# First of four convolutions computed directly ahead of a composed filter, in a two-layer style-convolution kernel

## The reference, cut to what matters

```
x = x + ffn0(cond0(x, style))      # ffn0 is a product with a 1024 x 1024 matrix
x = x + ffn1(cond1(x, style))      # ffn1 adds a gated low-rank part (LoRA experts)

cond: four convolutions of 3 taps, 64 -> 64 channels, in a row:
  same (1024) -> upsample x2 and blur [1,3,3,1] -> same -> blur and downsample x2
each: s = style @ mw.T + mb
      weight = SCALE * w * s[:, None, :, None]
      weight *= rsqrt(sum(weight * weight) + EPS)     # one factor per sample and output channel
      out = conv(x, weight) + bias
```

## Time and profile before

| what | value |
|---|---|
| time, median of 3 runs | 1484.66 us |
| profiled execution: span of its instructions | 1481.5 us |
| PE / weight loads (PEld) busy | 98% / 93% |
| DVE / ACT / POOL busy | 67% / 49% / 31% |
| granted PE clock | 1.00 of full speed but for the opening (0.91 from 20 to 40 us) |
| DMA | 145 MB, 36% of 16 queues' span |

### The profile page before, as it was taken

One profiled execution on the slowest core, in us unless ns is written; L12 is line 12 of the kernel. 1 busy time (PEld: TensorE's weight loads), 2 busy tenths in 40 slices (PEclk: granted clock), 3 DMA queues, 4 the chain that ended last, 5 costly groups with the idle time before them and its releaser, 6 DMA issues.

```text
span 1481.5 us, 28220 instructions
## 1 busy us (share of the span) xinstructions
PE 1457.1 (98%) x9619; PEld 1370.7 (93%) x9619; DVE 992.7 (67%) x2355; ACT 719.4 (49%) x1618; POOL 465.1 (31%) x542
## 2 busy tenths in 40 slices
PE   6999999999999999999989999999999999999999
PEld 4889898988988898889879999999999999999998
DVE  8766667766566655555676677677677677677674
ACT  5455445555544554455444445445454454454452
POOL 4133233323323332333313233233233233232230
PEclk9999999999999999999999999999999999999999
DMA  6443433443243234323533423423424424324322
GB/s 134 108 110 77 114 101 78 114 116 101 72 114 104 80 101 113 106 76 101 142 122 78 113 69 100 113 65 104 113 60 110 112 58 113 109 61 113 107 63 71
DMA packets 56635, 145.14 MB, mean 98 GB/s; under 512 B 19365, under 2 KB 21861, under 8 KB 56586
## 3 DMA queue, kind: packets, MB, share of 16 engines
q1 hardware_dynamic: 55928, 144.19, 36.2%
q10 hardware_dynamic: 658, 0.30, 0.1%
HBM read 110.92 MB, written 33.55 MB: 98 GB/s over the span
## 4 chain that ended last, share of the span: by engine, by line
PE 95%; DVE 3%; DMA 0%; issue 0%; SPq 0%; POOL 0%; ACT 0%; DVEq 0%; POOLq 0%; ACTq 0%
PE bank L1564 48%; PE bank L1416 13%; PE bank L1418 13%; PE bank L1417 13%; PE bank L1724 4%; PE bank L1596 1%; PE bank L1585 1%; PE bank L1629 1%; PE bank L1658 0%; DMA ends<-in_x_dram 0%; DVE win L1159 0%; DVE mtmp L1158 0%; PE bank L1741 0%; PE bank L1647 0%; DVE fw_l L1153 0%
## 5 line engine op out<-in xcount | busy, mean ns | idle before, releaser
L1564 PE MATMUL bank<-fw_h,ct_h 128*128 128x354 f32 (+2 forms) x1256 | 448.0, 357 | 0.8 <-DVE xout L1124 0.8
L1564 PE MATMUL bank<-fw_l,ct_h 128*128 128x354 f32 (+2 forms) x1256 | 445.1, 354 | 0.0
L1564 PE MATMUL bank<-fw_h,ct_l 128*128 128x354 f32 (+2 forms) x1256 | 443.2, 353 | 0.0
L414 POOL COPY conv_buf<-edge 128x4 f32 (+1 forms) x128 | 21.2, 193 | 848.9 <-DVE tw L1251 835.0
L1564 PEld LDWEIGHTS bank<-fw_h,ct_l 128*128 128x128 f32 x1256 | 236.1, 188 | 21.3
L1564 PEld LDWEIGHTS bank<-fw_h,ct_h 128*128 128x128 f32 x1256 | 236.7, 188 | 17.6 <-DVE ct_l L1275 0.9
L1564 PEld LDWEIGHTS bank<-fw_l,ct_h 128*128 128x128 f32 x1256 | 236.5, 188 | 15.5
L405 POOL TENSOR_TENSOR d_l<-d_f,d_h 128x512 fp32r<-128x512 f32 x128 | 154.8, 1209 | 102.4 <-ACT d_h L634 102.2
L1416 PE MATMUL bank<-d_h,tw 128*128 128x256 f32 x640 | 181.8, 284 | 0.3 <-DVE beta L974 0.3
L1418 PE MATMUL bank<-d_h,tw 128*128 128x256 f32 x640 | 180.5, 282 | 0.0
L1417 PE MATMUL bank<-d_l,tw 128*128 128x256 f32 x640 | 180.0, 281 | 0.0
(11 more groups left out here) (246 smaller groups left out, 3114.6 us busy)
## 6 DMA issues: line engine op xcount, KB each, us to landing
xraw<-in_x_dram SPq DMA_DIRECT2D x32, 512.0 KB, 6.6
xres<-in_x_dram SPq DMA_DIRECT2D x32, 512.0 KB, 4.2
x_dram<-xout SPq DMA_DIRECT2D x32, 512.0 KB, 2.9
xraw<-x_dram SPq DMA_DIRECT2D x32, 512.0 KB, 6.4
xres<-x_dram SPq DMA_DIRECT2D x32, 512.0 KB, 4.4
xraw<-in_x_dram SPq DMA_DIRECT2D x32, 511.5 KB, 8.0
xraw<-x_dram SPq DMA_DIRECT2D x32, 511.5 KB, 7.9
out_dram<-xout SPq DMA_DIRECT2D x31, 512.0 KB, 2.9
```

The costliest lines, as they stand in the source:

```text
L1564: last = mm(ffn_ps[e][:, 0:cols.stop - cols.start], ctf((ct_h, ct_h, ct_l)[part], k), (fw_h, fw_l, fw_h)[part][:, k, cols], start=k == beg ...
```

## The change

The first convolution is taken out of the composition and run over the sample by itself (`stage_mix`): two blocks of 128 rows, three matmuls of 512 columns each, so six matmuls of 512 columns a sample, into the whole of `conv_ps[h]`. `stage_t` goes. The composed filter holds the other three convolutions. It has seven taps in four slots (`NSH = 4`) and so six tap products of 256 columns a sample in `stage_conv` instead of eight.

The input of the filter is now the first convolution's result. ACT scales `xraw` by the style factor into a new tile `sig` (`x_scale`), casts its high part into the memory of `d_h` (`x_high`), POOL makes the low part (`split_low`); after `stage_mix` ACT scales PE's result back into `sig` (`mix_scaled`); POOL makes differences of it (`differ`), ACT the high parts (`y_high`), POOL the low parts (`lows`), and only then `stage_conv` can run. The filter's tile `t_f` is copied from PE's result by ACT (`f_high`) and DVE (`f_low`) with no scale, and has its own memory. A new list `x_take` puts ACT's scaling of the next pair between `t_high` and `sum_scaled`. SP's loads of `xraw` wait for `x_scaled`. In the opening of layer 0 DVE's `ends_2` and the third `prep_bias` change places, and the first `stage_conv` waits for all three biases.

```diff
-NSH = 5
+NSH = 4
...
+def halves(j, h, mixed=False):
+    return 4 * j + 2 * mixed + h + 1
...
                 def turn(j, first=False):
-                    sp.wait_ge(s["x_ready"], 2 * j)
+                    sp.wait_ge(s["x_scaled"], 2 * j)
                     load_x(ly, j)
...
+                def differ(h):
+                    m0, m1 = (sig[:, h, at:at + HL].rearrange("p (n e) -> p e n", e=2) for at in (0, 1))
+                    return nc.gpsimd.tensor_tensor(d_f[h][:, :, :], m0, m1, ALU.subtract)
+                def lows(h):
+                    nc.gpsimd.tensor_tensor(d_l[h][:, :, 1:QL + 1], d_f[h][:, :, :], d_h[h][:, :, 1:QL + 1].bitcast(F32), ALU.subtract)
+                    return nc.gpsimd.tensor_tensor(o_l[h][:, 1:QL + 1], sig[:, h, 1:HL:2], o_h[h][:, 1:QL + 1].bitcast(F32), ALU.subtract)
...
+                        pool.wait_ge(s["x_hi"], halves(j, h))
+                        nc.gpsimd.tensor_tensor(x_l[h], sig[:, h, :], x_h[h].bitcast(F32), ALU.subtract).then_inc(s["x_ready"], 1)
+                def mixed(j):
+                    for h in range(2):
+                        pool.wait_ge(s["y_made"], 2 * j + h + 1)
+                        differ(h).then_inc(s["d_made"], 1)
+                    for h in range(2):
+                        pool.wait_ge(s["x_hi"], halves(j, h, True))
+                        lows(h).then_inc(s["x_ready"], 1)
...
+            def x_scale(ly, j, h, before=None):
+                act.wait_ge(s["x_load"], 32 * j + 32)
...
+                    act.wait_ge(before["s"]["x_ready"], halves((j if before is ly else NPAIR) - 1, h, True))
+                nc.scalar.activation(sig[:, h, 0:HL], xraw[:, h, 0:L:2], ACT.Copy,
+                                     scale=ly["s_all"][:, 0, bass.ds(2 * j + h, 1)]).then_inc(s["x_scaled"], 1)
...
+                def mix_scaled(j, h):
+                    act.wait_ge(s["conv_acc"], halves(j, h))
+                    nc.scalar.activation(sig[:, h, 0:HL], conv_ps[h][:, :], ACT.Copy,
+                                         scale=lam1[:, bass.ds(2 * j + h, 1)]).then_inc(s["y_made"], 1)
...
-                    z_high(j)
+                    mix_scaled(j, 0)
+                    mix_scaled(j, 1)
+                    y_high(j, 0)
+                    f_high(j)
+                    y_high(j, 1)
                     t_high(j)
...
+                    x_take(j, 0, last)
+                    x_take(j, 1, last)
...
                 def t_low(j):
                     for h in range(2):
-                        v.tensor_scalar(full[:, 0:NSH, :], comp_ps[h][:, 0:NSH * C].rearrange("p (u c) -> p u c", c=C),
-                                        s_all[:, 0, bass.ds(2 * j + h, 1)], None, ALU.mult).then_inc(s["g_made"], 1)
...
+                        dve.wait_ge(s["f_dve" if h else "f_act"], 2 * j + 2)
+                        v.tensor_tensor(t_f[h][:, G0:SLOTS, :], t_f[h][:, 0:3, :], t_f[h][:, 1:4, :], ALU.add).then_inc(s["g_made"], 1)
...
+                def stage_mix(j, h, first=False):
+                    pe.wait_ge(s["x_ready"], halves(j, h))
+                    if not first:
+                        pe.wait_ge(s["ct_ready"], 4 * j)
...
+                    for i in range(2):
+                        at = slice(i * P, i * P + P)
+                        last = three(conv_ps[h][:, :], w1_h[:, at], w1_l[:, at], x_h[h][:, i:i + HL], x_l[h][:, i:i + HL], not i, bool(i))
+                    last.then_inc(s["conv_acc"], 1)
...
-                    for i, slot in enumerate((G0, G1, 4)):
+                    for i, slot in enumerate((G0, G1)):
...
                 def body(j, step=None):
                     stage_v(j)
                     ffn(ly, j - 1, 0, 9)
+                    stage_mix(j, 0)
+                    stage_mix(j, 1)
+                    ffn(ly, j - 1, 9, 12)
                     stage_u(j)
-                    ffn(ly, j - 1, 9, 19)
-                    stage_t(j)
-                    ffn(ly, j - 1, 19, 33)
+                    ffn(ly, j - 1, 12, 33)
                     stage_conv(j, 0)
                     stage_conv(j, 1)
...
                     ffn(ly, j - 1, 0, 13)
+                    stage_mix(j, 0)
+                    stage_mix(j, 1)
+                    ffn(ly, j - 1, 13, 17)
                     if not composed:
                         stage_u(j)
-                    ffn(ly, j - 1, 13, 28)
-                    if not composed:
-                        stage_t(j)
-                    ffn(ly, j - 1, 28, 49)
+                    ffn(ly, j - 1, 17, 49)
```

More of the change, by code:

```diff
@@ L360, in _ @@
                 if not n:
-                    sp.wait_ge(second["s"]["x_ready"], 2)
+                    sp.wait_ge(second["s"]["x_scaled"], 2)
                     load_x(second, 1)
@@ L455, in _ @@
                     ends_0()
-                for i, (full, hi, lo) in enumerate(((w3_st, w3_h, w3_l), (dn_st, dn_h, dn_l), (w1_st, w1_h, w1_l))):
-                    if i == 1 and not ly["lora"]:
-                        neighbours(0)
+                for i, (full, hi, lo) in enumerate(((w3_st, w3_h, w3_l), (sta[:, 4:8, :], w1_h, w1_l), (dn_st, dn_h, dn_l))):
                     pool.wait_ge(s["split_hi"], i + 1)
@@ L469, in _ @@
                 else:
-                    pool.wait_ge(s["t_ready"], 2)
-                    pool.wait_ge(s["t_side"], 2)
-                    neighbours(1)
+                    split_low(0)
+                    mixed(0)
                     pool.wait_ge(s["edge_ready"], 1)
@@ L715, in _ @@
                     fw_high(0, 2)
+                    x_high(ly, 0, 0)
+                    x_high(ly, 0, 1)
                     act.wait_ge(zs["scales_made"], 1)
                     v_high(0)
-                    x_high(ly, 0, 0)
-                    x_high(ly, 0, 1)
                     prep_m4(ly, (0, 1))
-                    z_high(0)
+                    act.wait_ge(zs["scales_made"], 2)
+                    mix_scaled(0, 0)
+                    mix_scaled(0, 1)
+                    f_high(0)
+                    y_high(0, 0)
+                    y_high(0, 1)
                     t_high(0)
@@ L1137, in _ @@
                         v.memset(tw[h][half(0), :, 0, 1, :].bitcast(F32), 0.0)
-                    v.memset(z_f[half(1), :, 3, :], 0.0)
+                    for h in range(2):
+                        v.memset(t_f[h][half(1), 3, :], 0.0)
                     link(v.memset(bb[:, :].bitcast(F32), 0.0))
@@ L1708, in stage_conv @@
                     last.then_inc(s["p_acc"], 1)
-                    if not first:
-                        pe.wait_ge(s["ct_ready"], 4 * j)
-                    elif not ly["lora"] and not h:
-                        pe.wait_ge(s["bias_ready"], 3)
-                    for i, slot in enumerate((0, 2, 4)):
-                        conv_tap(h, conv_ps[h][:, 0:QL], slot, d_h[h][:, 0, i:i + QL], d_l[h][:, 0, i:i + QL], i == 0, i == 2)
-                    for i, slot in enumerate((1, 3)):
-                        last = conv_tap(h, conv_ps[h][:, QL:2 * QL], slot, d_h[h][:, 1, i:i + QL], d_l[h][:, 1, i:i + QL], False, i == 1)
+                    for e in range(2):
+                        for i in range(2):
+                            last = conv_tap(h, conv_ps[h][:, e * QL:(e + 1) * QL], 2 * i + e, d_h[h][:, e, i:i + QL],
+                                            d_l[h][:, e, i:i + QL], not e and not i, i == 1)
```

214 lines of the change are left out of this document (104 added, 110 removed).

## The result

The changed kernel takes 1527.93 us (median of four runs, 1527.05 to 1532.84) against 1484.77 for the kernel before beside it (four runs, 1483.17 to 1485.86): +43.2 us, a ratio of 1.0299 (95% interval 1.0282 to 1.0316). The forecast was 1504 (+19.5): the direction is right, and less than half of the loss was seen.

The account below looks back on a forecast made before the run. PE, busy 98% of the span, was taken as the bound. On a span of 1481.5: -4 for PE's work, +20 hold at the filter run, +3 opening, 1500.5; with 3.2 to the median, 1504 us. Range 1481 to 1538 (by bounds 1484 to 1524).

Parts of the forecast that it names:

- PE's own work: PE's matmuls per pair: stage_t and two taps go, stage_mix comes; 0.06 us less a pair, -4 us over 64 pairs.
- the hold at the filter tile: Filter run: DVE's tile work held behind POOL; PE waits 0.45 us a body in layer 0, 0.2 in layer 1: +20 us.
- the opening: Opening of layer 0: the third bias comes after ends_2 and PE's first filter run waits for it: +3 us (0 to +5).
- the turn: PE's transposes of conv_buf: no term in the sum; rival 2 found 0.3 to 0.4 us to spare at 0.72 per scale.
- rival 2: At the turn ACT becomes the bound if each x_scale takes 0.5 us more: 0.6 a body, 1525 to 1545, chance 0.15.
- Its sign: What would show rival 2 in the profile: PE's transposes of conv_buf wait; no size given.
- the sum's own range: Range by the bounds of the terms around the forecast of 1504: 1484 to 1524 us.
- Rival 3: Mix matmuls on PE cost other than the ffn's: 0.01 us each is 8 us; no separate chance, the rest has 0.02.
- the 0.25 more of cover: Layer 1, between mix and filter run: 7.12 us of PE work against 6.87, so a wait of 0.2 (0 to 0.5).
- A difference: POOL's new differences of the mix result, reading with a step of 8 bytes: 1.27 us each (1.20 to 1.32).
- the low parts by themselves: POOL's low parts before the filter run: 2.07 us a sample, 4.1 for two, ending at 11.75 even alone.
- DVE adds 0.87 (614.28 to 615.07 and a tail): 18.7: Rival 2's step at the turn: after ACT's second sum at 17.8 DVE ends at 18.7; PE wants it at 19.0.

Follow-up runs that it names:

- e5: POOL's low parts (d_l, o_l) cut to two columns, on the changed kernel with w2_l after both conv_out: 1487.33 us, ratio 1.0021 to the kernel before.
- e1: Changed kernel, with DVE making the next pair's w2_l after both conv_out instead of between them: 1498.77 us, ratio 1.0102 to the kernel before.
- e3: Changed kernel, with ACT scaling the next pair's x after the first sample's sum and w2_high instead of ahead of them: 1499.03 us, ratio 1.0099.
- e2: Changed kernel, DVE's order left, with POOL making the next pair's x_l only after both conv_out of this pair: 1499.81 us, ratio 1.0105.
- e7: Changed kernel with x scaled after the first sum, two ffn matmuls moved ahead of the filter run, third bias before ends_2: 1486.43 us, ratio 1.0017.
- e6: Third bias ahead of ends_2, on the changed kernel with w2_l after both conv_out and two ffn matmuls moved: 1487.66 us, ratio 1.0027.

## Why the prediction was wrong

In the forecast's own terms the loss is: PE's own work -2 (forecast -4), the hold at the filter tile +9.6 (+20), the opening +3.8 (+3), and the turn +32, for which the sum had no term (by rival 2's sum 0.3 to 0.4 was to spare there). That makes 43.4, against 43.2 by the medians and 44.7 by the spans. The range of 1481 to 1538 holds 1528, and so does rival 2's band (1525 to 1545, chance 0.15), but by luck: that band came from `x_scale` at 1.2 us each. Its sign, PE's transposes of `conv_buf` that wait, did appear, but the hold of `w2_l` gives the same sign. By the bounds that it names, the sum's own range would begin at 1481, not at 1484.

**PE's own work: right in sign, half the size.** Mix matmuls start 0.233 apart (0.231 forecast). Undisturbed bodies are 21.11 (e5) and 22.27 us (e1), 0.02 and 0.04 less than before: -2 us, not -4. Rival 3 falls.

**The hold at the filter tile: right in kind, half the size.** PE wanted the tile at 12.45 in the body above (648.39, with the body's start at 635.94; forecast 12.42); it came at 12.54 (forecast 12.85) and PE was 0.31 late (forecast 0.45). In layer 1 the 0.25 more of cover sufficed: 0, not 0.2. The sum is 9.6 us, not 20. POOL's rows in that body, and then two where DVE had made the tile long before (pair 1 of layer 1), say which term was mis-sized:

```profile
642.60 1.04 POOL L404 TENSOR_TENSOR d_f<-sig 128x512 f32<-128x512 f32 x1 [0.37 <-ACT sig L686]
643.60 1.20 POOL L408 TENSOR_TENSOR d_l<-d_f,d_h 128x512 fp32r<-128x512 f32 x1
...
645.59 1.31 POOL L408 TENSOR_TENSOR d_l<-d_f,d_h 128x512 fp32r<-128x512 f32 x1
```

```profile
805.53 1.19 POOL L408 TENSOR_TENSOR d_l<-d_f,d_h 128x512 fp32r<-128x512 f32 x1
806.67 0.75 POOL L409 TENSOR_TENSOR o_l<-sig,o_h 128x256 fp32r<-128x256 f32 x1
```

The low parts begin 7.66 into the body (643.60), as forecast (7.65), but by luck. A difference takes 1.04, not 1.27, less than its lower bound of 1.20; but the second one waits 0.37 for ACT's second `mix_scaled`, a wait for which the prediction has no term, so the quicker row gains nothing. From there POOL took 4.39 us to the end of its last low part (647.99); the forecast was 4.1 and 0.6 for what DVE gets in between. The 0.6 was right: the two samples' `o_l` took 0.87 and 1.13 and the second `d_l` 1.31, where 0.75 and 1.19 are the rows with no DVE subtraction or addition let in. The mis-sized term is the low parts by themselves: 3.75 for the four (805.53 to 809.28), not 4.1. `o_l` was priced by a row that read `xraw` with a step of 16 bytes; it now reads `sig` with 8.

The 1.20 that was taken as a floor for the difference is a packed subtraction, but one that writes fp32r; no run here tells what the type of output costs by itself. The Trainium skill's GPSIMD Engine Reference (Performance pitfalls for Q7 kernels) had the direction right: with a step of 8 bytes in place of 16 the row fell from 1.32 to 1.04, so 16 was 27% dearer, where the page says half as much again. The page's figure is per element and ours is for the whole row, and a row is more than its elements (256 columns of `o_l` take 0.75, more than half of the 1.04 or 1.20 of 512), so the two need not differ.

**The turn: the step that failed.** Rival 2's sum put ACT's second sum at 17.8 and PE's wish at 19.0; they came at 17.5 and 18.9. `x_scale` was 0.75 (0.72 forecast; the rival had 0.5 more):

```profile
L605 ACT ACTIVATE sig<-xraw,s_all 128x512 f32<-128x512 f32 x128 | 90.3, 752 | 4.7 <-POOL o_l L409 1.6 <-issue 0.5
L686 ACT ACTIVATE sig<-bank,lam 128x512 f32<-128x512 f32 x128 | 88.0, 689 | 212.6 <-PE bank L1467 212.6
```

So ACT was in time for the second sum (rival 2 falls, as e3 shows), and the sentence "DVE adds 0.87 (614.28 to 615.07 and a tail): 18.7" is the error. It priced `conv_out` alone and left out what stands ahead of it on DVE: the `w2_l` pair, which had moved into the same microsecond as POOL's new x_l row. With it `conv_out` ended at 19.4. This cost some 31 us (32.0 of lateness at the turn, less the 0.9 that e1 leaves); e1, e2 and e3 each gave back 28 to 29. The row that would have shown it was in hand: the 1.53 us pair at 1102.44 is this very `w2_l`, held by POOL in this very place. The prediction used it to price the hold at the tile and did not ask why it cost nothing there. The trace of before answers:

```profile
1104.29 0.47 DVE L1268 SCALAR_TENSOR_TENSOR conv_buf<-bank,lam,conv_buf 128x254 f32<-128x254 f32 x1
```

```profile
1105.05 1.03 PE L1724 MATMUL bank<-ident,conv_buf 128*128 128x128 f32 x8
```

`conv_out` ended at 1104.76, and the second four transposes were wanted at 1105.05 + 0.43 = 1105.48: 0.7 to spare. The same place in layer 1 of the changed kernel, DVE and then PE:

```profile
1204.84 0.48 DVE L1315 SCALAR_TENSOR_TENSOR conv_buf<-bank,neg,conv_buf 128x254 f32<-128x254 f32 x1 [0.75 <-ACT conv_buf L726]
...
1207.60 0.47 DVE L1317 SCALAR_TENSOR_TENSOR conv_buf<-bank,lam,conv_buf 128x254 f32<-128x254 f32 x1
```

```profile
1206.95 0.60 PE L1771 MATMUL bank<-ident,conv_buf 128*128 128x128 f32 x4
1208.12 0.66 PE L1771 MATMUL bank<-ident,conv_buf 128*128 128x128 f32 x4 [0.57 <-DVE conv_buf L1317]
```

Counted from the start of the filter run (1097.42 before, 1200.75 after), `conv_out` ended at 7.34 before and ends at 7.32 now. But the filter run is 12 matmuls shorter, so the turn begins at 6.20 instead of 7.63: the 1.4 us by which PE comes sooner turn 0.7 to spare into 0.7 too late. The other part is the two `x_scale` (1.4 us) ahead of ACT's first sum: without its wait for that sum (0.75) `w2_l` would come ahead of POOL's row, as it does in e3.

The rule of the Trainium skill's SBUF — State Buffer (Who interferes with whom) holds at this place in both directions: `w2_l`, with two SBUF inputs, is held (1.40 for the second one); `conv_out`, whose first input is in PSUM, is not (0.47).

**The opening: right.** Forecast +3 (0 to 5). The first ffn matmul starts at 61.19 instead of 57.37: +3.8. The reason given, the third bias behind `ends_2`, holds too: e6 takes 4 to 5 back.

**What is left.** Of e7's 2.9 us the places seen are the opening (the first ffn matmul at 58.59 instead of 57.37), 3.1 us of lateness in layer 0 and the change of layers (69.82 instead of 68.38 from filter run to filter run), less the 2 of PE's own work. They were not tested further.

## What to carry to other kernels

When a contention is priced at one place, list every place where the two engines will now run at the same time, with what stands in order behind each held instruction. A held row of before that cost nothing had slack behind it, and the change can use that slack up; so ask of each such row how much was to spare. Work that the change takes off one engine can be the cover of another: here the shorter filter run took 1.4 us of it. Reordering alone (two scalings later, two ffn matmuls earlier, a bias earlier) gave back 41 us of 43 here.

## What was not expected of the hardware

Which of two engines pays is decided by some hundredths of a microsecond: with DVE's second `w2_l` 0.02 to 0.03 ahead it takes 0.34 and POOL's two rows 2.73; at 0.01 ahead (pair 11) it takes 1.47 and POOL's rows 2.60; with POOL 0.10 ahead it takes 1.40 and POOL's rows 2.65. One kernel ran the one way in 20 bodies and the other way in nearly all the rest, with 0.6 to 0.8 us of PE's time between them. And POOL's subtraction over 512 columns took 1.04 us with an fp32 result and a read step of 8 bytes, less than the 1.20 of a packed one with an fp32r result.
